# A decayed-neighbour sum: the layernorm ahead of the chain, and a new plan of units, marks and beats

## The chip, the cores and the metric

One core of one Trainium2 chip runs the kernel. The metric is device time in microseconds (us); less is better. One profiled execution is read beside it.

## The reference

`x` is 4096 x 64, `adj` a 4096 x 4096 matrix of zeros and ones (one in 256 is a one), `weight` 64 x 64, `bias` 64.

```
h       = maximum(layernorm(x), 0)
support = h @ weight
mask    = adj != 0
rank    = cumsum(mask, axis=1)
deg     = rank[:, -1:]
k       = minimum(deg, 100)
pos     = rank - (deg - k)
w       = mask * where(pos > 0, 0.5 ** (k - pos), 0)
out     = x + (w @ support + bias)
```

So each row's last neighbour counts with weight 1, the one before it with 1/2, and so on: a weight is a power of two whose exponent is the number of neighbours further right.

## The kernel before, in words

The 4096 rows are 32 tiles n of 128 rows (row `q * 32 + n` on partition q). A tile's adjacency is loaded by GpSimd as bf16 into `adj_b` (`load`, LOADS buffers), VectorE turns it into 0/1 bytes (`mask`, L310, RING buffers), and the columns are dealt into 32 steps of 128 columns (`column(n, t)`).

Tiles are taken in 18 units u of SIZES[u] tiles. The columns of a tile are cut into CHAINS[u] runs (2, or 4 for the first and the last unit) that are counted side by side, so a unit has STEPS[u] = 16 or 8 steps. In PSUM (`chain[u % 3]`) the unit holds for each row and column the exponent of the weight. `base(u)` (L549) puts in how many neighbours stand behind each run; that comes from VectorE's three halvings (`halve_1` to `halve_3`, L316 and L344) and a scan for each tile (`scan`, L353). Each step then adds the neighbours of 128 columns by a matmul of the mask with a diagonal (`count`, L563). ScalarE (`weigh`, L266) turns the counters into bf16 powers with one Relu whose integer result is read as bf16 bits.

MARKS[u] says how many of the unit's tiles are marked. In a marked tile the own neighbour's mark is added in the step and taken off in the next (`diag_past`, L561: one matmul more a step), and the power is the weight as it is. In an unmarked tile the powers of two steps are subtracted by VectorE: for BATCH steps together `floor` (L362) raises the small ones and `differ` (L369) subtracts neighbours; that saves TensorE's L561.

`product(u, s, k, h)` (L570) multiplies the powers by `support` (three bf16 parts of 64 columns, high, middle and low) into `acc[u % 4]`. VectorE then adds the three parts and x (`add_low`, `add_middle`, `add_high`), and SyncE stores the rows.

The order is written out by hand in slots g. Unit u has its base in slot STARTS[u], one step a slot after that, and its products LAGS[u] slots after the start; up to three units are in flight (FLIGHT). In a slot TensorE goes over c = 0, 1, 2: base or waits, then products and counts in turn. A count waits for ScalarE's powers of the unit's last step, so a unit makes one step a slot at most. Each engine has its own loop over the slots; VectorE's prepares masks and scans 9 to 2 slots ahead of a unit's start.

The layernorm: VectorE sums rows of x, centers one half of them and GpSimd the other, ScalarE squares, VectorE sums the squares (`square_sums`), takes the reciprocal of ScalarE's root with one Newton step (`deviation`) and multiplies (`normalize`, L432). TensorE transposes the rows in slots 5 and 8 (`turn_h`, L514), ScalarE applies the Relu, TensorE multiplies by the weights in slots 6 and 9 (`make_support`, L524), and the three parts are taken out in turn (`part` on ScalarE, `take_off` on TensorE, L532). Unit 0's products wait for all of it (`low_ready`).

## Time and profile before

| | |
|---|---|
| median of 3 runs | 231.36 us (231.02 to 233.29) |
| the profiled execution | 232.5 us, of it the span 230.1 us |
| TensorE busy | 88% of the span |
| VectorE busy | 86% |
| ScalarE busy | 71% |
| GpSimd busy | 11% |

The span goes from the first to the last instruction; the time of an execution has 2.4 us more than the span. Busy shares are means over a start, a long middle and a tail.

### The profile page before, as it was taken

What the parts mean: (1) busy time and instruction counts of PE and PEld (TensorE: products, weight loads), DVE (VectorE), ACT (ScalarE), POOL (GpSimd) and SP (SyncE); (2) the same over time, 40 slices, a digit from 0 to 9 for tenths busy, and PEclk for the clock granted to TensorE, in tenths of its full rate; (3) what the DMA queues carried; (4) which work ended last, traced back from release to release, by engine and by line L of the source; (5) the groups of instructions that cost most, each with busy time, mean ns of one, the idle gap of its engine ahead of it and who ended that gap; (6) DMA issues with size and microseconds to landing.
All of it is one profiled execution on the core that took longest, in us unless ns stands there. A gap on an engine that the chain in (4) does not pass through costs nothing.

```text
span 230.1 us, 6364 instructions
## 1 busy us (share of the span) xinstructions
PE 201.8 (88%) x2768; PEld 196.3 (85%) x2768; DVE 197.7 (86%) x227; ACT 163.7 (71%) x303; POOL 26.0 (11%) x53
## 2 busy tenths in 40 slices
PE   0005898899999999999999999999999899899994
PEld 0004885899999999999999999999999789899993
DVE  1799999997799989999979999969999999677053
ACT  2203489767877988878887878887889798787610
POOL 8921000411000010110010001000000000000000
PEclk9999999999999999999999999999999999999999
DMA  5999999999999999999999999999700000000001
GB/s 182 227 214 194 215 216 216 216 216 216 212 215 216 215 214 211 215 219 216 215 215 219 218 214 220 212 218 218 158 20 3 11 3 14 0 14 3 11 14 29
DMA packets 8074, 36.11 MB, mean 157 GB/s; under 512 B 1648, under 2 KB 3440, under 8 KB 3952
## 3 DMA queue, kind: packets, MB, share of 16 engines
q0 software_dynamic: 4608, 33.56, 70.1%
q1 hardware_dynamic: 3136, 2.10, 3.5%
q8 instruction: 22, 0.36, 0.6%
q10 hardware_dynamic: 304, 0.07, 0.1%
q14 instruction: 4, 0.03, 0.0%
HBM read 68.22 MB, written 1.05 MB: 301 GB/s over the span
## 4 chain that ended last, share of the span: by engine, by line
PE 71%; DVE 17%; issue 4%; DMA 4%; ACT 3%; POOL 1%; POOLq 0%
PE acc L570 31%; PE chain L563 22%; PE chain L561 13%; DVE masks L310 6%; DMA adj_b<-in_adj 4%; DVE part L316 3%; DVE powers L369 2%; PE acc L524 2%; ACT support L255 2%; DVE powers L362 2%; PE chain L549 1%; PE acc L514 1%; ACT powers L266 1%; DVE later L353 1%; DVE sums L344 1%
## 5 line engine op out<-in xcount | busy, mean ns | idle before, releaser
L266 ACT ACTIVATE powers<-chain 128x512 int16<-128x512 f32 (+1 forms) x282 | 152.3, 568 | 39.3 <-PE chain L563 31.3
L570 PE MATMUL acc<-support,powers 128*128 128x192 bf16 x1024 | 167.5, 246 | 2.8 <-issue 1.3
L563 PE MATMUL chain<-diag_own,masks 128*128 128x128 bf16 x640 | 125.6, 231 | 0.0
L561 PE MATMUL chain<-diag_past,masks 128*128 128x128 bf16 x596 | 118.5, 224 | 3.0 <-ACT powers L266 2.9
L570 PEld LDWEIGHTS acc<-support,powers 128*128 128x128 bf16 x1024 | 101.1, 102 | 4.5 <-DVE powers L369 1.7
L563 PEld LDWEIGHTS chain<-diag_own,masks 128*128 128x128 fp8e3 x640 | 91.0, 147 | 0.0
L561 PEld LDWEIGHTS chain<-diag_past,masks 128*128 128x128 fp8e3 x596 | 84.8, 145 | 5.0 <-ACT powers L266 4.7
L310 DVE TENSOR_SCALAR masks<-adj_b 128x4096 uint8<-128x4096 bf16 x32 | 72.9, 2279 | 3.8 <-DMA adj_b<-in_adj 3.8
L563 PE MATMUL chain<-diag_step,masks 128*128 128x128 bf16 x384 | 62.2, 220 | 0.0
L563 PEld LDWEIGHTS chain<-diag_step,masks 128*128 128x128 fp8e3 x384 | 52.1, 145 | 0.0
L206 POOL DMA_DIRECT2D adj_b<-in_adj x32 | 18.7, 585 | 116.3 <-DVE masks L310 111.8
L369 DVE TENSOR_TENSOR powers<-powers 128x2048 bf16<-128x2048 bf16 (+1 forms) x20 | 28.5, 1423 | 0.0
L353 DVE TENSOR_TENSOR_SCAN later<-sums 128x257 bf16<-128x257 uint8 (+1 forms) x32 | 22.9, 721 | 0.4
L549 PE MATMUL chain<-diag_base,later 128*128 128x128 bf16 x68 | 7.1, 226 | 18.0 <-DVE later L353 18.0
L362 DVE TENSOR_SCALAR powers<-powers 128x2304 int16<-128x2304 int16 (+3 forms) x20 | 17.2, 862 | 6.2 <-ACT powers L266 6.2
L549 PEld LDWEIGHTS chain<-diag_base,later 128*128 128x128 bf16 x68 | 4.8, 103 | 18.0 <-issue 18.0
L316 DVE TENSOR_TENSOR part<-masks 128x2048 uint16<-128x2048 uint16 (+1 forms) x18 | 19.9, 1104 | 0.2
L379 DVE TENSOR_TENSOR sum_a<-acc,x_sb 128x128 f32<-128x128 f32 (+1 forms) x18 | 4.9, 272 | 12.0 <-PE acc L570 12.0
L344 DVE TENSOR_TENSOR sums<-part 128x512 uint16<-128x512 uint16 (+1 forms) x18 | 11.9, 663 | 0.5
L316 DVE TENSOR_TENSOR part<-part 128x1024 uint16<-128x1024 uint16 (+1 forms) x16 | 10.5, 654 | 0.1
L255 ACT ACTIVATE support<-acc 128x512 bf16<-128x512 f32 x12 | 6.8, 620 | 1.9 <-PE acc L524 1.9
L394 DVE TENSOR_REDUCE row_sum<-x_sb 128x16 f32<-128x1024 f32 x2 | 2.4, 1220 | 5.4 <-DMA x_sb<-in_x 5.4
(45 smaller groups left out, 53.0 us busy)
## 6 DMA issues: line engine op xcount, KB each, us to landing
adj_b<-in_adj POOLq DMA_DIRECT2D x32, 1024.0 KB, 30.3
x_sb<-in_x SPq DMA_DIRECT2D x2, 512.0 KB, 4.7
out<-x_sb SPq DMA_DIRECT2D x14, 64.0 KB, 2.6
out<-x_sb SPq DMA_DIRECT2D x4, 32.0 KB, 9.3
w<-in_L_gnn_weight ACTq DMA_DIRECT2D x2, 16.0 KB, 4.6
bias_b<-in_L_gnn_bias ACTq DMA_DIRECT2D x1, 32.0 KB, 4.5
```

Source lines behind the costliest of these rows:

```text
L206: pool.dma_start(adj_b[:, n % LOADS, :], adj_t[n]).then_inc(adj_loaded[n % LOADS], 16)
L266: nc.scalar.activation(powers[:, c, b, cols].bitcast(i16), chain[c][:, cols], ACT.Relu, bias=(MAX_NEIGH + 1) * STEP).then_inc(powers_ready ...
L310: nc.vector.tensor_scalar(masks[:, (n + SHIFT) % RING, :], adj_b[:, n % LOADS, :], 0.0, 1.0, ALU.not_equal, ALU.mult).then_inc(mask_ready, 1)
L316: return nc.vector.tensor_tensor(outs, at[:, :, 0:length], at[:, :, length:2 * length], ALU.add).then_inc(done, 1)
L344: nc.vector.tensor_tensor(runs_of(sums, sums_4, u)[:, :, 0:h * P], at[:, :, :, 0], at[:, :, :, 1], ALU.add).then_inc(sums_ready, 1)
L353: nc.vector.tensor_tensor_scan(runs_of(later, later_4, u)[:, k, ::-1], two[:, 0, ::-1], two[:, 1, ::-1], (OWN + STEP) / STEP if k < MARKS[ ...
L362: nc.vector.tensor_scalar(bits, bits, STEP, None, ALU.max).then_inc(floored[c], 1)
L369: nc.vector.tensor_tensor(before, before, after, ALU.subtract).then_inc(weights_ready[c], 1)
L549: last = nc.tensor.matmul(chain[c][:, at:at + P], behind[:, hs - 1 - h], diag_base[:, :], start=(k + h == 0), stop=False, skip_group_check ...
L561: nc.tensor.matmul(chain[c][:, at:at + P], column(n, t + 1), diag_past[:, :], start=False, stop=False, skip_group_check=True)
L563: return nc.tensor.matmul(chain[c][:, at:at + P], column(n, t), diag_own[:, :] if marked else diag_step[:, :], start=False, stop=True, ski ...
L570: return nc.tensor.matmul(acc[u % ACCS][:, k * 3 * D:(k + 1) * 3 * D], powers[:, u % FLIGHT, s + 1 if k < MARKS[u] else s, at:at + P], sup ...
```

## The change: what it does

- The plan: BATCH is 4 instead of 8, LOADS 8 instead of 7, RING 12 instead of 10. Each unit is marked whole or not at all, but for unit 5; the last four units are unmarked. STARTS and LAGS of the first units are shorter, most later starts are one slot later.
- GpSimd issues the load of tile 0 ahead of the constants. It doesn't center any more; VectorE centers both halves. The two halves of x are taken in runs of four rows instead of eight.
- The transposes, of centered rows that aren't normalized yet, stand on TensorE ahead of the slots, after 40 matmuls into `chain[0]` whose result isn't used (`keep_warm`). ScalarE squares the transposed rows as well, and TensorE sums the squares by a matmul with `pair_sum`, two columns of ones for the two rows of a pair (`sum_squares`).
- `make_support` of all four blocks stands in slot 1. VectorE multiplies what it gives in PSUM by 1/deviation (`scale`); the three parts are then taken in slots 1 to 6.
- `cen`, `h_t` and the squares lie in the room of `powers`, and the PSUM tiles are dealt anew.
- Bias is added to x in four quarters, in VectorE's slots 15, 24, 50 and 72. Halvings and scans stand one slot earlier.
- `signs` is added but not used (`SIGNED` is empty).

```diff
-    BATCH = 8
-    LOADS = 7
-    RING = 10
+    BATCH = 4
+    LOADS = 8
+    RING = 12
...
-    MARKS = [1, 1, 1, 2, 1, 2, 1, 1, 2, 1, 1, 2, 1, 1, 0, 0, 1, 1]
-
-    STARTS = [0, 5, 10, 15, 22, 28, 33, 39, 45, 50, 56, 62, 67, 73, 79, 84, 90, 96]
-    LAGS = [14, 10, 8, 11, 11, 11, 11, 11, 11, 11, 11, 11, 11, 11, 11, 11, 11, 8]
+    MARKS = [1, 1, 1, 2, 2, 1, 2, 2, 0, 2, 2, 0, 2, 2, 0, 0, 0, 0]
+
+    STARTS = [0, 5, 7, 13, 23, 29, 34, 40, 46, 51, 57, 63, 68, 74, 80, 85, 91, 97]
+    LAGS = [7, 6, 8, 11, 11, 11, 11, 11, 11, 11, 11, 11, 11, 11, 11, 11, 11, 8]
...
-        h_t = sb("h_t", [P, T // 2, P], fp32)
-
-        sq = adj_b[:, LOADS - 1, :].bitcast(fp32).rearrange("p (t d) -> p t d", d=D)
-        row_sum, mean, sq_sum, var_eps, std, rough, newton_a, newton_b, newton_c, rstd = (
...
+        own_room = powers[:, 2, :, :].rearrange("p s c -> p (s c)")
+        cen = own_room[:, 0:2 * T * D].bitcast(fp32).rearrange("p (t d) -> p t d", d=D)
+        h_t = own_room[:, 2 * T * D:4 * T * D].bitcast(fp32).rearrange("p (a b) -> p a b", b=P)
+        sq_t = powers[:, 1, :, :].rearrange("p s c -> p (s c)")[:, 0:2 * T * D].bitcast(fp32)\
+            .rearrange("p (a b) -> p a b", b=P)
...
-        turned = (acc[0], acc[1])
-        split = (acc[2], acc[3])
+        spare = pb("spare", [P, 512], fp32)
+        turned = (spare, chain[2])
+        split = acc
+        sq_sum = chain[1]
...
-            return tensor[:, :, :].rearrange("p (h e t) d -> p e h t d", h=2, e=2)[:, 1 - f]
+            return tensor[:, :, :].rearrange("p (r e t) d -> p e r t d", r=RUNS, e=2)[:, 1 - f]
...
-                if n == LOADS - 1:
-                    pool.wait_ge(sq_sum_ready, 2)
                 if n >= LOADS:
                     pool.wait_ge(mask_ready, n - LOADS + 1)
                 pool.dma_start(adj_b[:, n % LOADS, :], adj_t[n]).then_inc(adj_loaded[n % LOADS], 16)
...
+            load(0)
...
+            nc.gpsimd.memset(pair_sum[:, :], 1.0).then_inc(zeroed, 1)
...
-            for n in range(4):
+
+            nc.gpsimd.affine_select(out=pair_sum[:, :], in_=pair_sum[:, :], compare_op=ALU.is_ge, fill=0.0, base=0,
+                                    pattern=[[-D, 2]], channel_multiplier=1).then_inc(zeroed, 1)
+            pool.wait_ge(zeroed, 8)
+            nc.gpsimd.affine_select(out=pair_sum[:, :], in_=pair_sum[:, :], compare_op=ALU.is_ge, fill=0.0, base=D - 1,
+                                    pattern=[[D, 2]], channel_multiplier=-1).then_inc(consts_ready, 1)
+            for n in range(1, 4):
                 load(n)
...
-            pool.wait_ge(mean_ready, 2)
-            nc.gpsimd.tensor_tensor(half_of(cen, 1), half_of(x_sb, 1), spread(mean, 1),
-                                    ALU.subtract).then_inc(cen_ready[1], 1)
             for n in range(4, NT):
                 load(n)
...
+            def square(i):
+                act.wait_ge(h_turned, i + 1)
+                nc.scalar.activation(sq_t[:, 4 * i:4 * i + 4, :], turned[i % 2][:, :].rearrange("p (a b) -> p a b", a=4),
+                                     ACT.Square).then_inc(sq_ready, 1)
...
+            def part(i, s):
+
+                if s:
+                    act.wait_ge(part_taken[i], s)
+                else:
+                    act.wait_ge(scaled[i], 1)
+                nc.scalar.activation(steps_of(support[:, :, s, :], i),
+                                     split[i][:, :].rearrange("p (r two d) -> p r two d", two=2, d=D),
+                                     ACT.Copy).then_inc(part_ready[i], 1)
...
                 act.wait_ge(chain_ready[c], taken_until(u) + b + 1 - (MARKS[u] == SIZES[u]))
+                if u in (1, 2) and b <= 1:
+                    act.wait_ge(sq_sum_ready if u == 1 else support_ready, 4)
...
             square(0)
+            turn_h(0)
             square(1)
+            turn_h(1)
+            square(2)
+            turn_h(2)
+            square(3)
+            turn_h(3)
             root()
             for g in range(SLOTS):
-                if g == 5:
-                    turn_h(0)
-                    turn_h(1)
-                if g == 6:
-                    part(0, 0, high_ready)
-                    part(1, 0, high_ready)
-                if g == 7:
-                    part(0, 1, middle_ready)
-                    part(1, 1, middle_ready)
-                if g == 8:
-                    part(0, 2, low_ready)
-                    part(1, 2, low_ready)
-                if g == 8:
-                    turn_h(2)
-                    turn_h(3)
-                if g == 9:
-                    part(2, 0, high_ready)
-                    part(3, 0, high_ready)
-                if g == 10:
-                    part(2, 1, middle_ready)
-                    part(3, 1, middle_ready)
-                if g == 11:
-                    part(2, 2, low_ready)
-                    part(3, 2, low_ready)
                 for c in range(FLIGHT):
                     for u in range(c, NU, FLIGHT):
                         if 0 <= g - STARTS[u] <= STEPS[u]:
                             weigh(u, g - STARTS[u])
...
+                if g == 1:
+                    part(0, 0)
+                    part(1, 0)
+                if g == 2:
+                    part(2, 0)
+                    part(3, 0)
+                if g == 3:
+                    part(0, 1)
+                    part(1, 1)
+                if g == 4:
+                    part(2, 1)
+                    part(3, 1)
+                if g == 5:
+                    part(0, 2)
+                    part(1, 2)
+                if g == 6:
+                    part(2, 2)
+                    part(3, 2)
...
+                dve.wait_ge(xb_ready, 4 * (FIRST[u] + SIZES[u] - 1) // T + 1)
...
-            def normalize(f):
+            def scale(i):
+
                 dve.wait_ge(ln_step, 6)
-                dve.wait_ge(cen_ready[f], 1)
-                nc.vector.tensor_tensor(half_of(cen, f), half_of(cen, f), spread(rstd, f),
-                                        ALU.mult).then_inc(unit_rows, 1)
+                dve.wait_ge(support_ready, i + 1)
+                of_block = rstd[:, :].rearrange("p (r i two) -> p r i two", i=4, two=2)[:, :, 3 - i, :]
+                block_of = split[i][:, :].rearrange("p (r two d) -> p r two d", two=2, d=D)
+                nc.vector.tensor_tensor(block_of, block_of, of_block.unsqueeze(3).to_broadcast([P, RUNS, 2, D]),
+                                        ALU.mult).then_inc(scaled[i], 1)
...
             def add_bias(f):
+
                 dve.wait_ge(bias_loaded, 16)
-                dve.wait_ge(cen_ready[f], 1)
-                nc.vector.tensor_tensor(half_of(x_sb, f), half_of(x_sb, f),
-                                        bias_b[:, :].unsqueeze(1).unsqueeze(1).to_broadcast([P, 2, Q, D]),
+                rows = slice(f * T // 4, (f + 1) * T // 4)
+                nc.vector.tensor_tensor(x_sb[:, rows, :], x_sb[:, rows, :],
+                                        bias_b[:, :].unsqueeze(1).to_broadcast([P, T // 4, D]),
                                         ALU.add).then_inc(xb_ready, 1)
...
             row_sums(0)
+            means(0)
             row_sums(1)
-            means(0)
+            center(0)
             means(1)
-            center(0)
-            square_sums(0)
+            center(1)
             mask(0)
             halve_1(0)
-            square_sums(1)
             halve_2(0)
             halve_3(0)
             scan(0, 0)
+            mask(1)
             variance()
-            mask(1)
             halve_1(1)
             deviation()
+            scale(0)
             halve_2(1)
+            scale(1)
             halve_3(1)
             scan(1, 0)
-            normalize(0)
+            scale(2)
+            scale(3)
             mask(2)
             halve_1(2)
-            normalize(1)
             halve_2(2)
             halve_3(2)
             scan(2, 0)
             mask(3)
-            add_bias(0)
-            add_bias(1)
-            dve.wait_ge(xb_ready, 2)
             for g in range(SLOTS + 4):
                 for u in range(NU):
                     if MARKS[u] < SIZES[u] and g - STARTS[u] in range(BATCH + 1, STEPS[u] + 2, BATCH):
                         floor(u, (g - STARTS[u] - 1) // BATCH - 1)
-
+                if g == 15:
+                    add_bias(0)
+                if g == 24:
+                    add_bias(1)
+                if g == 50:
+                    add_bias(2)
+                if g == 72:
+                    add_bias(3)
                 for u in range(NU):
                     to = STARTS[u] - g
                     if u >= 3 and to == 9 and FIRST[u] > 3:
                         mask(FIRST[u])
                     if u >= 3 and to == 7 and SIZES[u] > 1:
                         mask(FIRST[u] + 1)
+                    if u >= 3 and to == 7:
+                        halve_1(u)
                     if u >= 3 and to == 6:
-                        halve_1(u)
-                    if u >= 3 and to == 5:
                         halve_2(u)
                     if u >= 3 and to == 4:
                         halve_3(u)
-                    if u >= 3 and to == 3:
+                    if u >= 3 and to == 4:
                         scan(u, 0)
-                    if u >= 3 and to == 2 and SIZES[u] > 1:
+                    if u >= 3 and to == 3 and SIZES[u] > 1:
                         scan(u, 1)
...
+            def keep_warm(times):
+
+                for _ in range(times):
+                    nc.tensor.matmul(chain[0][:, 0:P], minus[:, :], diag_step[:, :], start=True, stop=True,
+                                     skip_group_check=True)
...
             def turn_h(i):
 
-                pe.wait_ge(unit_rows, i // 2 + 1)
+                pe.wait_ge(cen_ready[i // 2], 1)
                 if i >= 2:
                     pe.wait_ge(h_t_ready, i - 1)
+                    pe.wait_ge(sq_ready, i - 1)
                 for q in range(4):
-                    t = 8 * BLOCKS[i] + 2 * q
                     last = nc.tensor.transpose(turned[i % 2][:, q * P:(q + 1) * P],
-                                               cen[:, t:t + 2, :].rearrange("p t d -> p (t d)"), ident_f[:, :])
+                                               pairs_of(cen[:, :, :], i)[:, q, :], ident_f[:, :])
                 last.then_inc(h_turned, 1)
+
+            def sum_squares(i):
+                pe.wait_ge(sq_ready, i + 1)
+                for q in range(4):
+                    t = 8 * q + 6 - 2 * i
+                    last = nc.tensor.matmul(sq_sum[:, t:t + 2], sq_t[:, 4 * i + q, :], pair_sum[:, :],
+                                            start=(q == 0), stop=True, skip_group_check=True)
+                last.then_inc(sq_sum_ready, 1)
 
             def make_support(i):
                 pe.wait_ge(weight_loaded, 32)
                 pe.wait_ge(h_t_ready, i + 1)
-                if i >= 2:
-                    pe.wait_ge(low_ready, i - 1)
                 for q in range(4):
-                    last = nc.tensor.matmul(split[i % 2][:, q * P:(q + 1) * P], h_t[:, 4 * BLOCKS[i] + q, :],
+                    last = nc.tensor.matmul(split[i][:, q * P:(q + 1) * P], h_t[:, 4 * i + q, :],
                                             w2[:, :], start=(q == 0), stop=True, skip_group_check=True)
-                last.then_inc(split_ready, 1)
...
+            def take_off(i, s):
+
+                pe.wait_ge(part_ready[i], s + 1)
+                nc.tensor.matmul(split[i][:, :].rearrange("p (r two d) -> p r two d", two=2, d=D), minus[:, :],
+                                 steps_of(support[:, :, s, :], i), start=False, stop=True,
+                                 skip_group_check=True).then_inc(part_taken[i], 1)
...
+                if u == 1:
+                    pe.wait_ge(ln_step, 1)
...
             def before_products(u, s):
                 c = u % FLIGHT
-                if u == 0 and s == 0:
-                    pe.wait_ge(low_ready, 4)
+                if u < ACCS and s < 8:
+
+                    pe.wait_ge(part_ready[s // 2], 3)
+                    if s == 0:
+                        pe.wait_ge(part_ready[u], 3)
...
             pe.wait_ge(consts_ready, 6)
+            keep_warm(40)
+            turn_h(0)
+            turn_h(1)
+            pe.wait_ge(consts_ready, 7)
+            sum_squares(0)
+            turn_h(2)
+            sum_squares(1)
+            turn_h(3)
+            sum_squares(2)
+            sum_squares(3)
             for g in range(SLOTS):
...
+                if g == 1:
+                    make_support(0)
+                    make_support(1)
+                    make_support(2)
+                    make_support(3)
+                if g == 2:
+                    take_off(0, 0)
+                    take_off(1, 0)
+                if g == 3:
+                    take_off(2, 0)
+                    take_off(3, 0)
+                if g == 4:
+                    take_off(0, 1)
+                    take_off(1, 1)
+                if g == 5:
+                    take_off(2, 1)
+                    take_off(3, 1)
```

## Rows read from the trace of the kernel before

**Rows 1.** The page: busy time, and two lines of the 40 slices

```profile
PE 201.8 (88%) x2768; PEld 196.3 (85%) x2768; DVE 197.7 (86%) x227; ACT 163.7 (71%) x303; POOL 26.0 (11%) x53
...
PEclk9999999999999999999999999999999999999999
DMA  5999999999999999999999999999700000000001
```

**Rows 2.** Stretches: length, busy time (instructions) by engine, granted clock, DMA share, GB/s

```profile
100.00:120.00 20.00, 19.97 (x295) 19.83 (x293) 18.27 (x20) 16.55 (x29) 1.59 (x3) 1.00 1.03 216
...
180.00:190.00 10.00, 8.55 (x121) 8.26 (x121) 9.90 (x11) 8.21 (x16) 0.00 (x0) 1.00 0.03 8
190.00:200.00 10.00, 9.12 (x133) 8.98 (x132) 8.34 (x11) 8.26 (x15) 0.00 (x0) 1.00 0.03 8
```

**Rows 3.** Waits of the whole span: total us, times, longest

```profile
DVE sum_a L379 <- PE acc L570: 12.0, 6, 6.0
DVE powers L362 <- ACT powers L266: 6.2, 5, 2.2
...
PEld acc L570 <- DVE powers L369: 1.7, 3, 1.2
```

**Rows 4.** VectorE in order of time: start, length, instruction, wait before it

```profile
6.62 1.22 DVE L394 TENSOR_REDUCE row_sum<-x_sb 128x16 f32<-128x1024 f32 x1 [0.38 <-DMA x_sb<-in_x]
...
11.82 2.31 DVE L310 TENSOR_SCALAR masks<-adj_b 128x4096 uint8<-128x4096 bf16 x1 [0.29 <-DMA adj_b<-in_adj]
...
16.62 1.23 DVE L353 TENSOR_TENSOR_SCAN later<-sums 128x513 bf16<-128x513 uint8 x1
...
30.15 2.27 DVE L310 TENSOR_SCALAR masks<-adj_b 128x4096 uint8<-128x4096 bf16 x1
...
34.72 2.29 DVE L310 TENSOR_SCALAR masks<-adj_b 128x4096 uint8<-128x4096 bf16 x1
...
39.77 1.28 DVE L353 TENSOR_TENSOR_SCAN later<-sums 128x257 bf16<-128x257 uint8 x2
```

**Rows 5.** TensorE in order of time, to 43 us

```profile
27.10 0.31 PE L561 MATMUL chain<-diag_past,masks 128*128 128x128 bf16 x1
27.20 0.31 PE L563 MATMUL chain<-diag_own,masks 128*128 128x128 bf16 x1
...
27.52 2.81 PE L524 MATMUL acc<-w,h_t 128*128 128x128 f32 x16
...
35.05 2.02 PE L524 MATMUL acc<-w,h_t 128*128 128x128 f32 x16 [0.28 <-issue]
...
43.02 0.39 PE L549 MATMUL chain<-diag_base,later 128*128 128x128 bf16 x4
```

**Rows 6.** TensorE in order of time: unit 6's base and the last matmuls

```profile
72.94 0.39 PE L549 MATMUL chain<-diag_base,later 128*128 128x128 bf16 x4
...
219.71 7.05 PE L570 MATMUL acc<-support,powers 128*128 128x192 bf16 x80
```

**Rows 7.** VectorE in order of time: tile 10's mask and unit 6's second scan

```profile
62.78 2.29 DVE L310 TENSOR_SCALAR masks<-adj_b 128x4096 uint8<-128x4096 bf16 x1 [1.42 <-DMA adj_b<-in_adj]
...
71.48 0.69 DVE L353 TENSOR_TENSOR_SCAN later<-sums 128x257 bf16<-128x257 uint8 x1
```

**Rows 8.** Groups by form: count, busy us, mean ns, idle before

```profile
L369 DVE TENSOR_TENSOR powers<-powers 128x2048 bf16<-128x2048 bf16 x16 | 19.4, 1211 | 0.0
...
L369 DVE TENSOR_TENSOR powers<-powers 128x4096 bf16<-128x4096 bf16 x4 | 9.1, 2274 | 0.0
...
L432 DVE TENSOR_TENSOR cen<-cen,rstd 128x1024 f32<-128x1024 f32 x2 | 2.4, 1207 | 0.0
```

**Rows 9.** ScalarE in order of time, around 42 and 47 us

```profile
42.00 0.66 ACT L266 ACTIVATE powers<-chain 128x256 int16<-128x256 f32 x2 [0.29 <-PE chain L563]
...
46.76 1.15 ACT L266 ACTIVATE powers<-chain 128x512 int16<-128x512 f32 x3 [0.61 <-PE chain L563]
```

**Rows 10.** GpSimd in order of time: the first four loads

```profile
3.54 2.27 POOL L206 DMA_DIRECT2D adj_b<-in_adj  x4
```

**Rows 11.** The stretch from 5 to 6 us, columns as in Rows 2

```profile
5.00:6.00 1.00, 0.00 (x0) 0.00 (x0) 0.97 (x1) 0.00 (x0) 1.00 (x3) 1.00 1.23 397
```

More of the change, by code:

```diff
@@ L140, in gnn_decay_kernel @@
         std_ready = sem("std_ready")
-        unit_rows = sem("unit_rows")
         h_turned = sem("h_turned")
         h_t_ready = sem("h_t_ready")
-        split_ready = sem("split_ready")
-        high_ready = sem("high_ready")
-        middle_ready = sem("middle_ready")
-        low_ready = sem("low_ready")
+        support_ready = sem("support_ready")
+        scaled = [sem(f"scaled{i}") for i in range(4)]
+        part_taken = [sem(f"part_taken{i}") for i in range(4)]
+        part_ready = [sem(f"part_ready{i}") for i in range(4)]
         xb_ready = sem("xb_ready")
+        signs_ready = sem("signs_ready")
         mask_ready = sem("mask_ready")
@@ L246, in turn_h, with signs @@
                 act.wait_ge(h_turned, i + 1)
[L247 to L248 removed]
+                nc.scalar.activation(h_t[:, 4 * i:4 * i + 4, :], turned[i % 2][:, :].rearrange("p (a b) -> p a b", a=4),
                                      ACT.Relu).then_inc(h_t_ready, 1)
[L251 to L256 removed]
+            def part(i, s):
[6 more added lines that the diff above has]
+                                     ACT.Copy).then_inc(part_ready[i], 1)
+            def signs(n, j):
+                act.wait_ge(adj_loaded[n % LOADS], 16 * (n // LOADS + 1))
+                if n >= RING:
+                    u = UNIT_OF[n - RING]
+                    act.wait_ge(chain_ready[u % FLIGHT], taken_until(u) + TAKEN[u])
+                at = slice(j * N // PIECES, (j + 1) * N // PIECES)
+                nc.scalar.activation(masks[:, (n + SHIFT) % RING, at].bitcast(i8), adj_b[:, n % LOADS, at],
+                                     ACT.Sign).then_inc(signs_ready, 1)
             def weigh(u, b):
@@ L300, in _ @@
                             weigh(u, g - STARTS[u])
+                for n in SIGNED:
+                    if 0 <= g - SIGNED[n] < PIECES:
+                        signs(n, g - SIGNED[n])
+                if g == 1:
[16 more added lines that the diff above has]
+                    part(3, 2)
         @block.vector
@@ L305, in mask @@
             def mask(n):
+                if n in SIGNED:
+                    dve.wait_ge(signs_ready, PIECES * (1 + sum(m < n for m in SIGNED)))
+                    two = masks[:, (n + SHIFT) % RING, :].bitcast(u16)
+                    nc.vector.tensor_scalar(two, two, 0x0101, None, ALU.bitwise_and).then_inc(mask_ready, 1)
+                    return
                 dve.wait_ge(adj_loaded[n % LOADS], 16 * (n // LOADS + 1))
@@ L520, in make_support @@
                 pe.wait_ge(h_t_ready, i + 1)
-                if i >= 2:
-                    pe.wait_ge(low_ready, i - 1)
                 for q in range(4):
-                    last = nc.tensor.matmul(split[i % 2][:, q * P:(q + 1) * P], h_t[:, 4 * BLOCKS[i] + q, :],
+                    last = nc.tensor.matmul(split[i][:, q * P:(q + 1) * P], h_t[:, 4 * i + q, :],
                                             w2[:, :], start=(q == 0), stop=True, skip_group_check=True)
-                last.then_inc(split_ready, 1)
-            def take_off(i, s, ready):
-                pe.wait_ge(ready, i + 1)
-                t = 8 * BLOCKS[i]
-                nc.tensor.matmul(split[i % 2][:, :].rearrange("p (t d) -> p t d", d=D), minus[:, :],
-                                 support[:, t:t + 8, s, :], start=False, stop=True,
-                                 skip_group_check=True).then_inc(split_ready, 1)
+                last.then_inc(support_ready, 1)
+            def take_off(i, s):
[3 more added lines that the diff above has]
+                                 skip_group_check=True).then_inc(part_taken[i], 1)
             def column(n, t):
```

62 lines of the change are left out of this document (16 added, 46 removed).

## The prediction

> **What bounds the kernel now.** Read the page's engine line and slices first, then the stretches, the waits, and the order of time at the start. TensorE is busy 201.8 us of 230.1, VectorE 197.7 [rows 1]. From 43 us on TensorE is full: 295 matmuls start in 20 us [rows 2], 0.068 us each. It has gaps again only late, 1.45 us between 180 and 190 and 0.88 between 190 and 200, with 121 and 133 matmuls where 147 would fit; counted in missing matmuls that is 26 and 14, so 2.7 us. Three of those waits are for the differences of L369 [rows 3]. So the end is set by when TensorE gets full, by the number of its matmuls after that, and by about 3 us that VectorE's late differences cost.
>
> Before 43 us TensorE is badly used. The first tile is there at 11.82, its scan starts at 16.62 [rows 4], and the chain of unit 0 starts when it is done; the layernorm's transposes and the support matmuls stand in the middle of it (L524 takes 2.81 and 2.02 us) [rows 5]. Unit 3, the first with two tiles, gets its base at 43.02 [rows 5], unit 6 at 72.94, and the last matmul ends at 226.76 [rows 6].
>
> Two suppliers stand close behind TensorE. The DMA slices are full up to about 160 us [rows 1]: the mask of tile 10 waits 1.42 us for its load and starts at 62.78, and unit 6's second scan at 71.48, 0.8 us before what it makes is used at 72.94 [rows 7]. VectorE waits 12.0 us for accumulators and 6.2 for ScalarE's powers in the whole run, part of it at the tail [rows 3]; between 180 and 190 it is busy 9.90 of 10 [rows 2].
>
> **Part 1: the layernorm goes ahead.** Removed from VectorE before its loop: two square sums, two normalizations of 1.21 us [rows 8] and the two bias additions, the 2.3 us between the end of mask 3 (30.15 and 2.27) and mask 4 at 34.72 [rows 4]. Added: the second centering (1.2, from GpSimd) and four scalings of 128x512 from PSUM. No row shows these; half of a 128x1024 multiplication is 0.60 [rows 8], the other bound is a whole one, 1.21; by size I take 0.65, so 2.6 in all. Walking VectorE's order with x landing as now (second row sum at 6.62): centerings to 10.3, mask 0 at 11.3 if tile 0 lands a little earlier than now, its scan done at 15 to 16 (now 17.85), mask 1 from about 16 (landing) to 18.5, variance at 18.6. The bias additions turn up in the loop as four of about 0.65, where the masks wait for loads anyway; if that cover is gone they cost what they cost now, 2.3 us.
>
> On TensorE, ahead of the slots: 16 transposes, moved (a record each, so by L524's rows 2.0 to 2.8 us), and 16 sums of squares, two records each as L524 has for a product in full precision. The latter's price is not shown; L524 is the nearest (16 records in 2.81 us at first, 2.02 later) and bounds 32 of them to 4.0 to 5.6 us from above, as its moving tile has 128 columns and theirs 2; half of it bounds them from below, and I take 4. The PEclk slices read full speed everywhere [rows 1], yet in the first stretch consecutive 128-column matmuls start 0.10 us apart [rows 5], the 1.2 GHz level (128 / 1.2 GHz = 0.107), until 27.3, after which they stand about 0.06 apart, the 2.4 GHz level; the engine had worked back to back from 24.7. The 40 matmuls of keep_warm cost 40 x 0.107 = 4.3 us and lie in idle time, from constants at about 4.4 to 8.7, ahead of the first centering at 9. So layernorm ends on TensorE between 15 and 19.5 by the clock level; the variance is needed at 18.6, so most of that is covered.
>
> Then the supports: 32 records of L524, 4.0 us at the fast level, 5.6 at the slow, before slot 2. They start after unit 0's first count at about 17, so slot 2 starts at 21 to 22.5 where its like stood at 19.7. ScalarE then has a weighing and two parts in each of slots 1 to 6, 0.6 + 2 x 0.5 and two hand-overs, about 1.8 us a slot: slot 7, unit 0's first products, at about 32. Slots 7 and 8 run at the rate of a four-run chain with products between, 1.15 + 0.61 = 1.76 [rows 9], slots 9 to 13 hold two single-tile units at 0.66 + 0.29 = 0.95 [rows 9], taken as 1.05 for the products between: unit 3's base comes at 32 + 3.5 + 5.2 = 40.7 less about 1 for the overlap of the first slots, 39.7. It came at 43.02. Its supply: tiles 0 and 10 were masked as they landed, at 11.82 [rows 4] and 62.78 [rows 7], so one lands every 5.1 us and tile 4 at 32.2; mask, three halvings and two scans take 6.3 (34.72 to 39.77 and 1.28) [rows 4], so 38.5. Both ends meet.
>
> **Part 2: starts and marks.** At unit 3's base 140 matmuls are done instead of 120, at unit 6's 562 instead of 536, of 2712 in the loop (2710 before). From unit 3 to unit 6 there are 21 slots: ten of 1.45 (unit 3's chain without a unit's products in its way: 1.76 less four products of 0.08, for the 80 that end the run take 7.05 with a stall in them [rows 6]), and eleven that average 1.62 (three of unit 4's and 5's pace at 1.76, the rest lighter): 14.5 + 17.8 = 32.3. Unit 6's base then comes at 72.0, against 72.94. Supply bounds it at 69.1: mask 10 from 62.78 and 6.3 us of work, so DMA doesn't forbid it. The gain of unit 3 is largely given back here, as the loop is bound by the chain through ScalarE with two units in flight; what remains is that more work lies behind.
>
> After unit 6's base: before, 2176 matmuls in 226.76 - 72.94 - 3.1 = 150.7 us, 0.0693 each; after, 2152, so 149.1. The sum of past-run matmuls hardly changes (596 to 598), since 20 tiles are marked in both; they only move from the end to the middle.
>
> **Part 3: four beats.** With eight beats, the second batch's floor is issued two slots before its products; with four, six slots before (unit 17: three). The late waits, 2.7 us and 0.3 in the tail, should nearly go; I leave 0.7. The price is 26 floors and 26 differences for 20 of each. A doubled difference takes 1.21 for 2048 and 2.27 for 4096, so 0.15 us is what one more costs: 12 x 0.15 = 1.8 us on VectorE over 60 us of slots, covered as fewer unmarked tiles (5 for 7) lie before unit 14. The Trainium skill, "VectorE: DVE Perf Modes", section "The TRN2 errata", gives a fixed 58 cycles in its table and says that about 150 is measured; this case's rows give 0.15 us, which is the latter, and by the table the price would be 0.7 us.
>
> **Part 4: first load ahead.** The load of tile 0 is issued at about 0.95 instead of 3.54 [rows 10]. x is still moving then: between 5 and 6 us 397 GB/s move [rows 11], against 216 with tiles alone [rows 2], and x's second half is there at 6.62 [rows 4]. A gain of at most 2.6 us on tile 0's landing; for the stream behind it only the bytes' order changes, since the DMA is full from 3 us on, so I give it 0.5. A loss is possible: the row sums wait for x. Sharing evenly would set x back by as long as its own megabyte takes at that rate, 2.6 us; up to 1.5 us are absorbed, as mask 1 would have waited for its load anyway. I take that. The 1 KB runs of x (2 KB before) are inside it.
>
> **Sum.** 72.0 + 149.1 + 0.7 = 221.8 for the last matmul, 226.76 before; 3.3 us to the end as before: span 225.1, 5.0 less. The profiled execution took 232.5 with a span of 230.1, so 227.5; the median shown is 1.1 below the profiled time: 226.4.
>
> **Rivals.** (a) x comes late by a tile. If tile 0's rows (5.1 us a tile) go before x's second half on the DMA engines, that half lands at 11.7, VectorE's start moves by 5.1 less the 1.5 absorbed, and the median is 226.4 + 3.6 = 230.0, no change by measure. Against: the 397 GB/s of [rows 11] with both queued. Chance 0.16. The Trainium skill, "DMA: Bandwidth & Descriptors", section "Queues, rings and completion order", says that a DMA engine takes turns between queues and drains a whole packet before it switches; by that rule x would wait like this; no row here shows a mixed stretch long enough to tell. (b) The same place, but row by row: x's runs wait behind several tiles' rows. It decides for slower once x's second half lands after about 17 us: 1.5 absorbed, 5.0 of gain and 2.3 of measure beyond 6.6 + 1.5; at 20 us the time is 238. Chance 0.08. (c) The gaps late don't go: VectorE must stop at twice as many floors, and each costs up to the 1.2 of a late wait; the front's part alone, 2 us, gives 229.4, 0.08 with a bit of (a). (d) The front is quicker than I walked it: slot 7 at 30 and unit 3 bound by its supply at 38.5 or a little before; unit 6 at 70, median 224.3. Chance 0.18. The forecast keeps 0.50.
>
> **How the numbers follow.** A change under 1%, 2.3 us, is about what a measurement can't tell. Faster (under 229.0): forecast and (d), 0.68, and the lower half of (a) and (c), 0.06. Same: the rest of them, 0.17. Slower: (b) and a worse (c), 0.09. The range reaches from (d) to (a): 223.0 to 230.6.
>
> **What would show it.** Unit 3's base near 39.7 and unit 6's near 72; unit 0's slot 2 after 21; no TensorE gap over 0.5 us from 180 on; 26 floors; x's second row sum starting by 8.2. If that starts after 11, Part 4 is wrong; if unit 6's base is later than 74, Part 1 or 2; if waits for L369's differences remain above 1 us, Part 3.

## The result, and the profile after

The changed kernel takes 247.03 us (median of 4 runs, 246.58 to 247.13), the kernel before 231.77 beside it: a ratio of 1.065 (95% interval 1.059 to 1.070). It is slower, and rival (b) of the prediction is what happened.

The page of the changed kernel: busy time, two of its slice lines, and the chain that ended last by line.

```profile
PE 213.4 (87%) x2842; PEld 206.8 (84%) x2842; DVE 201.6 (82%) x242; ACT 161.2 (66%) x302; POOL 28.7 (12%) x55
...
PE   2500199988999999999999999999999999999994
...
DMA  6999999999999999999999999975000000000001
...
PE acc L630 35%; PE chain L623 25%; PE chain L621 14%; DMA x_sb<-in_x 11%; PE chain L575 3%; PE acc L583 2%; ACT powers L298 2%; ACT support L275 2%; PE chain L609 2%; PE spare L567 1%; PE chain L567 1%; DVE row_sum L436 0%; DVE powers L445 0%; SPq L204 0%; DVE sum_b L426 0%
```

11% of the chain (the work that ended last, followed back to its start) is the load of x; in the chain of the kernel before, DMA has 4% in all, and that is tiles. TensorE's slices show where: after keep_warm it has nothing to do until the fifth slice, 24 us in. VectorE in order of time says why; the row sums and the first mask answer to [rows 4]:

```profile
4.52 1.22 DVE L436 TENSOR_REDUCE row_sum<-x_sb 128x16 f32<-128x1024 f32 x1 [4.52 <-DMA x_sb<-in_x]
5.77 2.83 DVE L440 TENSOR_SCALAR mean<-row_sum 128x16 f32<-128x16 f32 x1
27.39 1.22 DVE L436 TENSOR_REDUCE row_sum<-x_sb 128x16 f32<-128x1024 f32 x1 [18.79 <-DMA x_sb<-in_x]
...
31.00 2.29 DVE L351 TENSOR_SCALAR masks<-adj_b 128x4096 uint8<-128x4096 bf16 x1
```

The second half of x is there at 27.39 instead of 6.62. What the DMA engines did meanwhile, queue by queue (packets, MB, share of the 16 engines' time), in the changed kernel from 10 to 20 us: q0 carries the tiles, q1 x, q10 the small loads of ScalarE's queue.

```profile
q0 software_dynamic: 226, 1.72, 88.9%
q1 hardware_dynamic: 227, 0.23, 8.5%
q10 hardware_dynamic: 109, 0.02, 1.0%
```

226 packets of tiles (rows of 8 KB but for a few that only signal) and 227 of x (runs of 1 KB): one for one. x gets half of the turns and 8.5% of the time. It is so on a small scale too: in the four single microseconds from 17 to 21 us the counts are 24 and 23, 25 and 25, 23 and 23, 25 and 25. The trace doesn't say which of the 16 engines moved a packet, but long blocks of rows followed by long blocks of runs wouldn't give this. 227 turns of x in 10 us on 16 engines are 0.7 us a turn. Up to 4.0 us 511 packets of x had started and 545 came after, 34 for each engine; at 0.7 us that is about the 23 us from there to 27.39. In the kernel before, the same view from 2 to 6.5 us:

```profile
q1 hardware_dynamic: 544, 1.05, 73.0%
q0 software_dynamic: 22, 0.18, 19.5%
q10 hardware_dynamic: 304, 0.07, 7.0%
```

There x was practically through when the first 22 rows of tiles began.

Behind its late start the changed kernel runs much as forecast. The bases of units 3 and 6, which answer to those of [rows 5, 6], and a late stretch with the columns of [rows 2]:

```profile
61.15 0.39 PE L609 MATMUL chain<-diag_base,later 128*128 128x128 bf16 x4
...
92.55 0.39 PE L609 MATMUL chain<-diag_base,later 128*128 128x128 bf16 x4
```

```profile
180.00:200.00 20.00, 20.00 (x298) 20.00 (x296) 19.89 (x22) 16.55 (x30) 0.00 (x0) 1.00 0.02 6
```

Unit 3 comes 18.1 us later than before and the span is 14.7 longer, so 3.4 us were won after the start. Unit 6 comes 19.6 us later: 1.5 us are lost between the two bases and 4.9 won behind unit 6. TensorE's late gaps are gone: 298 matmuls in 20 us, where 254 started between 180 and 200 before.

### The profile page after: what moved, and what is told of

It is laid out like the page before. It is cut to its first block, busy times and chain, and to the rows that moved or that the text cites. A ratio compares the mean times of both kernels' runs of the same rounds, so it can differ in the third digit from the quotient of the medians.

```text
span 244.8 us, 6605 instructions
## 1 busy us (share of the span) xinstructions
PE 213.4 (87%) x2842; PEld 206.8 (84%) x2842; DVE 201.6 (82%) x242; ACT 161.2 (66%) x302; POOL 28.7 (12%) x55
## 4 chain that ended last, share of the span: by engine, by line
PE 82%; DMA 11%; ACT 4%; DVE 1%; issue 1%; SPq 0%
PE acc L630 35%; PE chain L623 25%; PE chain L621 14%; DMA x_sb<-in_x 11%; PE chain L575 3%; PE acc L583 2%; ACT powers L298 2%; ACT support L275 2%; PE chain L609 2%; PE spare L567 1%; PE chain L567 1%; DVE row_sum L436 0%; DVE powers L445 0%; SPq L204 0%; DVE sum_b L426 0%
## 5 line engine op out<-in xcount | busy, mean ns | idle before, releaser
L298 ACT ACTIVATE powers<-chain 128x512 int16<-128x512 f32 (+1 forms) x279 | 149.9, 572 | 36.4 <-PE chain L623 35.4
L630 PE MATMUL acc<-support,powers 128*128 128x192 bf16 x1024 | 163.2, 246 | 1.6 <-ACT powers L298 1.3
L623 PE MATMUL chain<-diag_own,masks 128*128 128x128 bf16 x640 | 118.5, 228 | 0.0
L621 PE MATMUL chain<-diag_past,masks 128*128 128x128 bf16 x598 | 113.0, 223 | 1.0 <-ACT powers L298 0.5
L623 PEld LDWEIGHTS chain<-diag_own,masks 128*128 128x128 fp8e3 x640 | 89.2, 146 | 0.0
L623 PE MATMUL chain<-diag_step,masks 128*128 128x128 bf16 x384 | 57.0, 220 | 0.0
L219 POOL DMA_DIRECT2D adj_b<-in_adj x32 | 23.7, 746 | 132.8 <-DVE masks L351 131.9
L403 DVE TENSOR_SCALAR powers<-powers 128x2048 int16<-128x2048 int16 (+3 forms) x26 | 17.8, 684 | 7.7 <-ACT powers L298 7.6
L567 PE MATMUL spare<-ident_f,powers 128*128 128x128 f32 x8 | 2.2, 432 | 20.5 <-DVE powers L445 20.5
L567 PEld LDWEIGHTS spare<-ident_f,powers 128*128 128x128 f32 x8 | 1.6, 241 | 20.8 <-DVE powers L445 20.8
```

What stands on the lines that cost most here:

```text
L219: pool.dma_start(adj_b[:, n % LOADS, :], adj_t[n]).then_inc(adj_loaded[n % LOADS], 16)
L298: nc.scalar.activation(powers[:, c, b, cols].bitcast(i16), chain[c][:, cols], ACT.Relu, bias=(MAX_NEIGH + 1) * STEP).then_inc(powers_ready ...
L403: nc.vector.tensor_scalar(bits, bits, STEP, None, ALU.max).then_inc(floored[c], 1)
L621: nc.tensor.matmul(chain[c][:, at:at + P], column(n, t + 1), diag_past[:, :], start=False, stop=False, skip_group_check=True)
L623: return nc.tensor.matmul(chain[c][:, at:at + P], column(n, t), diag_own[:, :] if marked else diag_step[:, :], start=False, stop=True, ski ...
L630: return nc.tensor.matmul(acc[u % ACCS][:, k * 3 * D:(k + 1) * 3 * D], powers[:, u % FLIGHT, s + 1 if k < MARKS[u] else s, at:at + P], sup ...
```

## The experiments

Each was run beside the kernel before and has a profile. Ratios are to that kernel (231.4 to 233.5 us on the chips used), with 95% intervals.

**The load of tile 0 back behind the constants** (e1_load_behind).

```diff
-            load(0)
-            for n in range(1, 4):
+            for n in range(0, 4):
```

> The changed kernel with one part undone: the load of tile 0 stands behind the constants again, together with loads 1 to 3. Theory A (tile rows of 625 ns and x runs take turns one by one on the DMA engines, so x's second half waits for three to four tiles): x's second half lands at 6.5 to 7 instead of 27.4, the base of unit 3 moves by about 20 us to 42 or earlier, and the time is 226 to 229, below the kernel before. Theory B (x is late because it is cut into 1 KB runs, 64 for an engine instead of 32, wherever the load stands): x's second half still lands after 15 and the time stays above 238. Theory C (the new plan of units is slower by itself): x lands early, and the time is still above 233.

Measured 226.24 us, ratio 0.974 (0.970 to 0.978). The early load carries the whole loss: the rest of the change makes the kernel 2.6% faster. VectorE's first operations (with two of GpSimd), and the bases of units 3 and 6:

```profile
6.17 1.97 DVE L439 TENSOR_SCALAR mean<-row_sum 128x16 f32<-128x16 f32 x1
6.21 1.43 POOL L240 MEMSET sums<- 128x1542 uint16 x1
7.53 0.58 POOL L241 MEMSET sums<- 128x513 uint16 x1
7.90 1.22 DVE L435 TENSOR_REDUCE row_sum<-x_sb 128x16 f32<-128x1024 f32 x1
...
13.15 2.29 DVE L350 TENSOR_SCALAR masks<-adj_b 128x4096 uint8<-128x4096 bf16 x1 [1.56 <-DMA adj_b<-in_adj]
```

```profile
40.24 0.40 PE L608 MATMUL chain<-diag_base,later 128*128 128x128 bf16 x4 [0.28 <-DVE later L393]
...
71.62 0.39 PE L608 MATMUL chain<-diag_base,later 128*128 128x128 bf16 x4
```

Theory A holds; B falls, since the 1 KB runs are still there and x is in by 7.9. C falls too. The second row sum is 19.5 us earlier than in the changed kernel (7.90 for 27.39) and the time 20.8 us shorter. TensorE is quicker at the start as well: the first four transposes take 0.66 us and the supports 4.70, in the changed kernel, where keep_warm lies 20.5 us back, 1.12 and 5.73.

**The kernel before with tile 0's load first, and nothing else** (e2_before_load_first).

```diff
+            load(0)
             for m in (ident_f, minus, diag_own, diag_past, diag_step, diag_base):
...
-            for n in range(4):
+            for n in range(1, 4):
```

> The kernel before with one edit only: tile 0's load is issued ahead of the constants. Theory A: x has 32 runs of 2 KB for an engine instead of 64 of 1 KB; those left when the tile's rows begin at about 3.7 us (20 or so for an engine) then take about 0.7 us each, so x's second half lands at 15 to 18 us, and the time is 9 to 12 us longer than before, 241 to 244. Theory B: with 2 KB runs x lands within 2 us of the 6.6 of before, and the time is 230 to 233.

Measured 242.51 us, ratio 1.044 (1.041 to 1.046). The queues from 8 to 16 us, and the second row sum:

```profile
q0 software_dynamic: 183, 1.37, 86.0%
q1 hardware_dynamic: 184, 0.38, 13.7%
q10 hardware_dynamic: 182, 0.04, 2.3%
```

```profile
17.95 1.22 DVE L395 TENSOR_REDUCE row_sum<-x_sb 128x16 f32<-128x1024 f32 x1 [11.00 <-DMA x_sb<-in_x]
```

Three queues, 183, 184 and 182 packets: again one for one. The edit hurts in the kernel before as well, by 10.2 us (x is 11.3 us later, so 1.1 are absorbed), and half the number of runs for x (2 KB each) makes half of the delay: 11.3 us against 20.8.

**x in whole rows, the load of tile 0 still first** (e3_x_in_rows).

```diff
-            for f in range(2):
-                sp.dma_start(half_of(x_sb, f), half_of(x.rearrange("(p t) d -> p t d", t=T), f))\
-                  .then_inc(x_loaded[f], 16)
+            sp.dma_start(x_sb[:, :, :], x.rearrange("(p t) d -> p t d", t=T)).then_inc(x_loaded[0], 16)
...
-                dve.wait_ge(x_loaded[f], 16)
+                dve.wait_ge(x_loaded[0], 16)
```

> The changed kernel, load of tile 0 still first, but x is loaded by one DMA of whole rows: 128 runs of 8 KB, 8 for an engine, instead of two DMAs of 1 KB runs. Theory A: most of the 8 runs are through when the tile's rows begin, and the rest take turns with only a few of them, so x lands at 6.5 to 8.5 us and tile 0 at about 10; the time is 226 to 229. If instead the early load delays x by bytes and not by turns, x lands at 9.5 or later whatever the runs, and the time is above 229.

Measured 225.13 us, ratio 0.969 (0.966 to 0.971). All of x is in at 5.74, a little earlier than expected, and tile 0's mask starts at 11.25:

```profile
5.74 1.22 DVE L434 TENSOR_REDUCE row_sum<-x_sb 128x16 f32<-128x1024 f32 x1 [5.74 <-DMA x_sb<-in_x]
...
11.25 2.28 DVE L349 TENSOR_SCALAR masks<-adj_b 128x4096 uint8<-128x4096 bf16 x1
```

Same bytes, tile 0 first each time, another number of runs: 27.39, 17.95 and 5.74 us for runs of 1, 2 and 8 KB. The delay goes by turns, not by bytes. This edit also makes one DMA of two; e2_before_load_first has two as the changed kernel has, so between 1 and 2 KB it isn't that. The early load and the long runs together are worth about 1 us (226.24 to 225.13; the two intervals touch).

**Without keep_warm** (e4_no_warm), the line `keep_warm(40)` removed from e1_load_behind.

> As e1_load_behind, and the 40 matmuls of keep_warm are left out. If they bring the clock up for the layernorm's matmuls, these take some 4 to 8 us longer in all without them and the time is 2 to 5 us above e1_load_behind. If TensorE's wait for the first centering lets the clock fall again, or the stretch is covered by VectorE's masks, the difference is under 1 us.

Measured 228.78 us (227.09 to 229.98), ratio 0.986 (0.980 to 0.992). The warm-up is worth 2.5 us by the medians and 1.1 by the two profiled executions, in which unit 3's base is at 41.30 and 40.24. In these the first four transposes take 1.09 instead of 0.66 us and the supports 5.85 instead of 4.70; why two of the four runs without it take 229.9 is open. Most of the layernorm gets nothing of the warm-up, as the clock doesn't last. The granted clock of e1_load_behind, by stretch (length, TensorE busy and count, granted clock, DMA share, GB/s):

```profile
11.00:12.00 1.00, 0.66 (x7) 1.00 1.06 221
12.00:16.00 4.00, 4.00 (x22) 0.52 1.01 211
16.00:20.00 4.00, 4.00 (x23) 0.50 1.04 217
20.00:22.00 2.00, 2.00 (x14) 0.50 1.04 217
22.00:24.00 2.00, 2.00 (x18) 0.90 1.00 209
```

0.50 is the 1.2 GHz level. Before it TensorE had idled from 8.2 to 10.3 us, then run eight transposes at the fast level and the first of the two-column matmuls. In e4_no_warm the same column reads 1.00 from the start, with transposes of 1.09 us: there only the durations tell the level.

**GpSimd's clearing earlier** (e5_memset_early), on e3_x_in_rows: the two memsets of `sums` and `sums_4` right behind `load(0)`, and `keep_warm(24)`.

> As e3_x_in_rows, and GpSimd clears sums and sums_4 right behind the load of tile 0 instead of behind loads 1 to 3, with 24 instead of 40 matmuls of keep_warm since the constants come 2 us later. In e3_x_in_rows VectorE's first mean, 128x16, took 1.59 us (0.17 the second), and in the changed kernel 2.83, each up to the end of GpSimd's clearing. If the two engines stand in each other's way there, the mean takes under 0.4 us now, centering and transposes come 1.2 to 1.6 us earlier, and the time is 0.5 to 1.5 us below e3_x_in_rows, as mask 1 waits for its load anyway. If the mean waits for something else, it stays above 1 us and the time with it. Loads 1 to 3 come 2 us later, at 7.1, while tile 0 lands only at 9.7, which should cost nothing.

Measured 225.71 us (224.69 to 227.12), ratio 0.972 (0.966 to 0.978). The half on the mean is right, the half on the time is not:

```profile
6.99 0.18 DVE L438 TENSOR_SCALAR mean<-row_sum 128x16 f32<-128x16 f32 x1
```

```profile
9.48 1.11 PE L565 MATMUL spare<-ident_f,powers 128*128 128x128 f32 x4
```

The mean takes 0.18 instead of 1.59 us, so it was GpSimd's clearing that held it, and the transposes start 0.4 earlier; but 24 warm-up matmuls didn't bring the clock up: four transposes take 1.11 us, in e3_x_in_rows 0.66. Unit 3's base is at 39.82 against 39.39 there. The warm-up's cut took what the earlier clearing gave; mask 1, whose load is issued later here, also starts 0.2 us later (17.48 for 17.28).

**Eight beats in the new plan** (e6_eight_beats), on e1_load_behind: `BATCH = 8`, and the last entry of LAGS 11 for 8.

> As e1_load_behind, with differences over eight beats again (and unit 17's products 11 slots behind its start instead of 8, since a batch of eight needs them to be). The prediction gave four beats 2.3 us, the late waits of TensorE for differences: 228 to 229.5, with gaps of 0.5 to 1.2 us after 170 us in TensorE's row. If the marks alone have removed those waits (fewer differences before unit 14), the time stays within 1 us of e1_load_behind.

Measured 232.61 us (230.14 to 234.18, 10 runs), ratio 1.000 (0.997 to 1.003): 6.4 us above e1_load_behind by the medians and 6.0 by the ratios, well over twice what I expected. TensorE's waits for the differences (total, times, longest), and its busy time between 210 and 220:

```profile
PE acc L629 <- DVE powers L409: 4.8, 4, 1.8
...
PEld acc L629 <- DVE powers L409: 3.2, 2, 2.1
```

```profile
210.00:220.00 10.00, 7.48 (x95) 1.00 0.03 8
```

Not all of it is the beats. In the profiled execution the first four transposes take 1.10 us here and 0.66 in e1_load_behind, and unit 6's base is at 72.62 for 71.62: 1.0 of the 6.7 us between the two spans (230.6 and 223.9) is there at unit 6's base already. The rest, 5.7, is still far more than the 2.2 us of the old plan (next experiment), and the marks alone don't remove the late waits. That it is the four whole unmarked units at the end that make large batches so costly is likely but not shown, and part may be unit 17's later products, which this run can't separate.

**Four beats in the kernel before** (e7_before_four_beats), `BATCH = 4` and nothing else.

> The kernel before with differences over four beats and nothing else. If the late waits (2.7 us and 0.3 in the tail) came from the large batches, they go, and the time is 2 to 3 us below the kernel before. If the added 12 VectorE instructions weigh as much as the smaller batches bring, the time stays within 1 us.

Measured 229.88 us, ratio 0.990 (0.985 to 0.994): 2.2 us, within what was expected. The two late stretches of [rows 2], with 121 and 133 matmuls there:

```profile
180.00:190.00 10.00, 9.25 (x136) 1.00 0.03 8
190.00:200.00 10.00, 10.00 (x149) 1.00 0.03 8
```

15 and 16 matmuls more in the two stretches are 2.1 us at 0.068.

**The old marks, starts and lags** (e8_old_plan), on e1_load_behind.

> As e1_load_behind, with the marks, starts and lags of the kernel before: only the layernorm ahead, the order of loads and the four beats are left of the change. The prediction put the layernorm's gain at about 3 us at unit 3's base, largely through the shorter starts (slots 13 for 15, single-tile units closer together). With the old starts slots 7 to 14 hold less than two units, so unit 3's base comes 1 to 3 us later than in e1_load_behind and unit 6's as well: 228 to 230. If the time is within 1 us of e1_load_behind, starts and marks bring nothing and all of the gain is the layernorm's and the beats'.

Measured 227.72 us (227.07 to 229.79), ratio 0.982 (0.976 to 0.988). That is a little under the 228 to 230 expected. The interval overlaps that of e1_load_behind (0.970 to 0.978), so marks, starts and lags are worth somewhere between nothing and 3.5 us; the two profiled executions are 1.6 us apart. Unit 3's base is at 42.52 (40.24 in e1_load_behind), unit 6's at 72.16 (71.62). What is left in this kernel (the layernorm's move, four beats, more loads in flight, the later bias additions) brings most of the gain; these weren't taken apart.

**Fillers between the square sums** (e9_fill_squares), on e3_x_in_rows, and **variance ahead of mask 1 as well** (e10_variance_first).

```diff
                     t = 8 * q + 6 - 2 * i
+                    keep_warm(2)
```

```diff
-            mask(1)
             variance()
+            mask(1)
```

> As e3_x_in_rows, and two of keep_warm's matmuls stand ahead of each of the 16 square-sum matmuls, 32 more in all. In e1_load_behind the granted clock is 1.00 for the first transposes and 0.50 from about 12 to 22 us, in which the two-column matmuls run 0.21 us apart. If the clock falls because these matmuls give TensorE little to do, it stays up now: transposes of four take 0.6 instead of 1.09 us, the supports 4.1 instead of 4.7 or more, and the square sums end 1 to 4 us earlier, less the fillers' 1.8; the time is 0.5 to 2 us below e3_x_in_rows if VectorE's variance can use it, or equal if mask 1 sets it. If the clock falls all the same, the fillers cost 3.4 us on the path and the time is 1 to 3 us longer.

> As e9_fill_squares, and VectorE takes the variance ahead of mask 1 instead of behind it. In e3_x_in_rows mask 1 waits 1.04 us for its load and ends at 19.5, and the square sums are done at about 19.0. If the clock stays up in e9_fill_squares the squares are done at 16 to 17 and the weighings can start 2 us earlier: 0.5 to 2 us below e9_fill_squares. If the clock falls, VectorE stops for the squares until 20 or later, mask 1 starts after them, and the time is 1 to 2.5 us longer than e9_fill_squares.

Measured 225.11 (ratio 0.967, 0.963 to 0.971) and 225.02 us (0.967, 0.963 to 0.971), the same as e3_x_in_rows. Neither gain of 0.5 to 2 us came. The clock stays up through the square sums (e9_fill_squares, columns as above), and in e10_variance_first the variance is taken at 17.33 instead of 19.49:

```profile
12.00:16.00 4.00, 4.00 (x50) 1.00 0.93 175
16.00:20.00 4.00, 4.00 (x46) 1.00 1.04 217
```

```profile
17.33 0.19 DVE L448 TENSOR_SCALAR var_eps<-chain 128x32 f32<-128x32 f32 x1 [1.09 <-PE chain L574]
17.44 2.29 DVE L349 TENSOR_SCALAR masks<-adj_b 128x4096 uint8<-128x4096 bf16 x1
...
21.65 0.70 DVE L471 TENSOR_TENSOR acc<-acc,rstd 128x512 f32<-128x512 f32 x1
```

But the first scaling starts at 21.65, in e3_x_in_rows at 21.97: it stands behind mask 1 and its halving, and ScalarE waits 3.96 us for it. Faster square sums move the wait from TensorE to VectorE. And what is won doesn't last: in e10_variance_first ScalarE's second weighing starts 1.5 us earlier than in e3_x_in_rows (23.81 for 25.32), unit 0's first product only 0.2 (31.77 for 31.94). In between the last two scalings start 0.5 us earlier, not 1.5, and TensorE, which had been idle from 22 to 23 us, has a granted clock of 0.50 from 27 to 30 us in both of these kernels, where e3_x_in_rows has 1.00. The fillers move the slow stretch, they don't remove it. Units 3 and 6 get their bases at 39.23 and 70.63 in e10_variance_first (39.39 and 70.78 in e3_x_in_rows). Three kernels at 225.0 to 225.1 are the best found, 3.1 to 3.3% faster than the kernel before.

## Why the prediction was wrong

**The step that failed is in Part 4**: "Sharing evenly would set x back by as long as its own megabyte takes at that rate, 2.6 us". It took the DMA engines to share by bytes or time. In this trace they share by packets: of each turn of 0.7 us the 8 KB row has nearly all (88.9% of the time for 8.5%), and a 1 KB run waits for a whole row each time. x has 64 runs for each of 16 engines; half of them were left when the rows of tile 0 came, and each had to wait for a row. The delay is 27.39 - 6.62 = 20.8 us where Part 4 had 2.6, and the prediction's own sign for it, a second row sum after 11, came true. The changed kernel, e2_before_load_first and e3_x_in_rows show that the delay goes with the number of runs (64, 32 and 8 for an engine), e1_load_behind that it vanishes without the early load. The other term of Part 4, 1.5 us absorbed, was near: 1.1 in e2_before_load_first.

**Rivals (a) and (b).** The Trainium skill, "DMA: Bandwidth & Descriptors", section "Queues, rings and completion order", which rival (a) quotes, says that a DMA engine takes turns between queues and drains a whole packet before it switches. The trace agrees on the turns; I took a packet to be a whole tile's rows and priced one tile, and by the counts above a turn is one row or run. Rival (b) had the right mechanism and the right way to price it: it counts beyond 8.1 us, so with x at 27.4 it gives 226.4 + 19.3 = 245.7, measured 247.0. How late x would be it didn't work out; its example was 20 us. (Its bound for slower counts the absorbed 1.5 twice: 6.6 + 1.5 + 5.0 + 2.3 is 15.4, not 17.) It got a chance of 0.08, and the only argument against either rival is the 397 GB/s of [rows 11] "with both queued". That was wrong: the same queue view from 5 to 6 us, which I hadn't put beside it, has 165 packets of x and only 7 of tiles, so in that stretch the two hardly met. The range stopped at 230.6 and should have reached to rival (b).

**What was right**, all measured with the load behind the constants: unit 3's base at 40.24 (forecast 39.7), unit 6's at 71.62 (72.0), the time 226.24 (226.4). In the changed kernel itself: no gap over 0.5 us after 180, 26 floors. After unit 6's base e1_load_behind needs 148.9 us to the last matmul (220.52), the sum had 149.8.

**The number for the start was luck in part.** 39.7 for unit 3's base rests on two errors of Part 1 that cancel. TensorE's order has the base of unit 0 behind the square sums, so in e1_load_behind it comes at 19.68 and slot 2 starts at 25.03, not at 21 to 22.5; then slots 2 to 6 take 1.46 us each, not 1.8, and unit 0's first product is at 32.35 (forecast about 32). The square sums cost 0.21 us a record at the slow clock, 6.6 us for 32, where I took 4, and the variance came at 20.26, not 18.6. Tile 0 was masked at 13.15, not 11.3, and the first mean took 1.97 us instead of 0.17. The mean was covered, as VectorE waited another 1.56 us for the tile; the late tile was not, or not wholly: mask 1 starts at 18.07 without a wait, in e3_x_in_rows at 17.28, as its load lands. (The loop has 2714 matmuls, 2712 before, not 2712 and 2710; the 2152 and 2176 of the sum go by the right totals.)

**Part 3** was sized at 2.3 us, and 2.2 is what four beats bring in the kernel before. In the new plan they are worth up to 6.4, 5.7 by the profiles: plan and beats depend on each other, a link that the prediction didn't see.

**Part 2**: that much of unit 3's gain is given back by unit 6 holds (2.8 us ahead, then 1.3; forecast 3.3, then 0.9). With the old starts unit 3 is only 0.5 us ahead and unit 6 0.8 (e8_old_plan), so the shorter starts win 2.3 us at unit 3 and 0.5 of it is left at unit 6. How much marks, starts and lags bring by themselves stays open between 0 and 3.5 us.

## What to carry to other kernels

A bulk load issued early doesn't share bandwidth fairly with a small load that the start waits for: in these traces each run that the small load still has to move on a DMA engine costs it the duration of one row of the large load, so count the former and multiply by the latter. Load what the start needs first and in long runs, or let the bulk load wait. A forecast that comes out right in its total may hold two errors that cancel: check the steps in between too. And when a rule and a single high number in a stretch disagree, look at the queues' packets in that stretch before the chances are set.

## What the hardware showed that was not expected

- Three DMA queues took turns one for one whatever the size of the packets (e2_before_load_first): 183, 184 and 182 packets in 8 us, for 1.37, 0.38 and 0.04 MB.
- A 128x16 operation on VectorE takes 1.97 us in e1_load_behind (2.83 in the changed kernel) beside the end of GpSimd's load issues and its two clearings, and ends within 0.05 us of them. Moved apart it takes 0.18. A reduction of 128x1024 beside the clearing takes 1.22 as ever in the kernel before and in e4_no_warm; right behind the held mean it took 1.50 in e3_x_in_rows.
- The granted clock falls to 0.50 in a stretch in which TensorE is busy all the time, with two-column matmuls and fp32 transposes, and stays at 1.00 there with two bf16 matmuls of 128 columns ahead of each two-column product (e9_fill_squares), only to fall to 0.50 from 27 to 30 us.
- The clock line reads 1.00 ahead of the first rise too: in the kernel without warm-up no fall is shown, yet four transposes take 1.09 us, the length they have at 0.50 elsewhere.
